# Two correction branches a tile instead of four in the context product of a fused Perceiver layer

## The reference, cut to what matters

```python
def _L0_xattn_ref(x1, x2, x1_scale, x1_zp, x2_scale, x2_zp):
    def fake_quant(x, scale, zp):
        s = scale.reshape(())
        z = zp.reshape(())
        q = jnp.clip(jnp.round(x / s + z), QMIN, QMAX)
        return (q - z) * s
    q1 = fake_quant(x1, x1_scale, x1_zp)
    q2 = fake_quant(x2, x2_scale, x2_zp)
    return jnp.matmul(q1, q2)
...
x = x + _L0_xattn_ref(_layernorm(x, axis=-1), ctx_4096, L0_xattn_x1_scale, L0_xattn_x1_zp, L0_xattn_x2_scale, L0_xattn_x2_zp)
x = x + _L0_attn_ref(_layernorm(x, axis=-1), L0_attn_Wqkv, L0_attn_Wo)
x = x + _L0_ffn_ref(_layernorm(x, axis=-1), L0_ffn_weight, L0_ffn_bias, L0_ffn_gate_w, L0_ffn_in_channel_scale, L0_ffn_out_channel_scale)
```

## Time and profile before

| | us |
|---|---|
| median of three runs | 401.46 (401.28 to 401.50) |
| the profiled execution, its own time | 400.98 |
| its span, first instruction to last | 399.2 |
| PE busy | 357.8 (90%) |
| DVE busy | 312.6 (78%) |
| ACT busy | 254.0 (64%) |
| POOL busy | 133.2 (33%) |
| DMA, bytes moved | 91.56 MB, 229 GB/s on average |

### The profile page before, as it was taken

One profiled execution on the slowest core, in us unless ns is written; L12 is line 12 of the kernel. 1 busy time (PEld: TensorE's weight loads), 2 busy tenths in 40 slices (PEclk: granted clock), 3 DMA queues, 4 the chain that ended last, 5 costly groups with the idle time before them and its releaser, 6 DMA issues.

```text
span 399.2 us, 9987 instructions
## 1 busy us (share of the span) xinstructions
PE 357.8 (90%) x4141; PEld 231.7 (58%) x4141; DVE 312.6 (78%) x592; ACT 254.0 (64%) x306; POOL 133.2 (33%) x148
## 2 busy tenths in 40 slices
PE   0437967999789999999999999999999999999996
PEld 0113943774344784569655965588457847955444
DVE  6898798998946689768985898679867997584753
ACT  3857885866788767864886577675878365233221
POOL 5320033415241224512471236213722246143051
PEclk9999999999999999999999999999999999999999
DMA  7999999479999579775867576757685200100002
GB/s 303 410 372 410 408 406 409 142 262 411 312 407 367 220 203 410 298 227 128 316 222 248 154 270 221 298 159 259 245 315 159 30 2 2 57 0 2 2 2 105
DMA packets 30243, 91.56 MB, mean 229 GB/s; under 512 B 8112, under 2 KB 8496, under 8 KB 30192
## 3 DMA queue, kind: packets, MB, share of 16 engines
q1 hardware_dynamic: 28320, 84.42, 58.9%
q10 hardware_dynamic: 1872, 6.40, 4.2%
HBM read 85.05 MB, written 4.19 MB: 224 GB/s over the span
## 4 chain that ended last, share of the span: by engine, by line
PE 56%; DVE 18%; DMA 9%; ACT 7%; SPq 4%; issue 3%; POOL 1%; DVEq 0%; ACTq 0%; POOLq 0%
DMA ring<-ctx 9%; PE R L1691 8%; PE T L1507 6%; PE R L1452 4%; ACT b L603 4%; PE R L1454 4%; PE R L1453 4%; PE R L1543 4%; PE C L1488 4%; PE R L1546 4%; PE R L1545 4%; SPq L380 2%; PE T L1590 2%; PE R L1574 2%; DVE st L1005 2%
## 5 line engine op out<-in xcount | busy, mean ns | idle before, releaser
L603 ACT ACTIVATE b<-ring,quant,qpar 128x2048 uint8<-128x2048 f32 x61 | 126.4, 2093 | 14.3 <-DMA ring<-ctx 8.2
L1543 PE MATMUL R<-T_hi,Wqkv_hi 128*128 128x128 f16 x448 | 77.8, 220 | 0.0
L1545 PE MATMUL R<-T_lo,Wqkv_hi 128*128 128x128 f16 x448 | 77.5, 220 | 0.0
L1546 PE MATMUL R<-T_hi,Wqkv_lo 128*128 128x128 f16 x448 | 77.5, 219 | 0.0
L1488 PE MATMUL C<-b,aT 128*64 128x512 f16 x256 | 36.1, 414 | 11.9 <-ACT b L603 5.9
L337 POOL TENSOR_TENSOR Pr<-Pr,mx 128x512 f32<-128x512 f32 x20 | 20.7, 1043 | 75.5 <-DVE mx L1109 75.5
L494 POOL TENSOR_TENSOR Pr<-Pr,mx 128x512 f32<-128x512 f32 x32 | 35.4, 1117 | 29.1 <-DVE mx L1115 29.1
L1543 PEld LDWEIGHTS R<-T_hi,Wqkv_hi 128*128 128x128 f16 x448 | 43.9, 98 | 2.0 <-issue 0.2
L1545 PEld LDWEIGHTS R<-T_lo,Wqkv_hi 128*128 128x128 f16 x448 | 43.8, 98 | 0.1
L1546 PEld LDWEIGHTS R<-T_hi,Wqkv_lo 128*128 128x128 f16 x448 | 43.8, 98 | 0.0
L1691 PE MATMUL R<-sgn,XS_hi 128*128 128x512 fp8e4 x96 | 36.6, 381 | 0.0
(11 more groups left out here) (172 smaller groups left out, 856.5 us busy)
## 6 DMA issues: line engine op xcount, KB each, us to landing
ring<-ctx SPq DMA_DIRECT2D x64, 1024.0 KB, 6.6
ring<-L_attn_Wo SPq DMA_DIRECT2D x4, 1024.0 KB, 9.3
ring<-L_ffn_weight SPq DMA_DIRECT2D x4, 1024.0 KB, 4.9
Wo<-L_attn_Wqkv SPq DMA_DIRECT2D x7, 544.0 KB, 15.4
X<-x ACTq DMA_DIRECT2D x6, 512.0 KB, 4.1
out<-X ACTq DMA_DIRECT2D x6, 512.0 KB, 6.1
X<-x SPq DMA_DIRECT2D x2, 512.0 KB, 11.3
sgn<-L_attn_Wqkv SPq DMA_DIRECT2D x1, 544.0 KB, 18.4
```

What stands on the lines that cost most here:

```text
L603: e.activation(b8[:, c % BRING, :], ring[:, slot, :], ACT.Identity, scale=qR2, bias=qZ2).then_inc(s_rf[slot], 1)
L1543: e.matmul(dst, hi, rows[0], start=k == 0 and g == 0, stop=False, skip_group_check=True)
L1545: e.matmul(dst, hi, rows[1], start=False, stop=False, skip_group_check=True)
L1546: last = e.matmul(dst, lo, rows[0], start=False, stop=k == KT - 1, skip_group_check=True)
```

## The change

The branch stands in the odd pairs only, and holds the correction for that pair and for the one before: 48 matmuls, where each of two branches held 24. So a pair's slots of `b16` may not be written again before the *next* pair has passed its branch, if the pair is even. The new function `read_by(t, c)` gives the count of `s_ctx` that `conv(t, c)` waits for. For pieces 6 and 7 it is 4t + 2 where it was 4t + 1; for pieces 4 and 5 it is 4(t-1) + 4 where it was 4(t-1) + 3; for 0 to 3 it is what it was.

```diff
+        def read_by(t, c):
+            return t * 4 + 2 if c >= BRING else (t - 1) * 4 + (2 if c // 2 == 1 else 4)
...
-                before = (t - 1) * 4 + 4 if c < 2 else (t - 1) * 4 + c // 2 + 1
-                at_least(e, s_ctx, before if c < BRING else t * 4 + 1)
+                at_least(e, s_ctx, read_by(t, c))
...
-                e.wait_ge(s_ctx, t * 4 + 1 if c >= BRING else (t - 1) * 4 + c // 2 + 1)
+                e.wait_ge(s_ctx, read_by(t, c))
...
-                def products(k, lhs, first, last):
+                def products(k, lhs, first, last, of_pair=pair):
...
-                                           b16[:, (2 * pair + b) % BRING, k, n * HALF:(n + 1) * HALF],
+                                           b16[:, (2 * of_pair + b) % BRING, k, n * HALF:(n + 1) * HALF],
...
                 products(0, rows(0), pair == 0, False)
-
-                with e.If_ne(uneven, 0):
-                    for k in range(2):
-                        for part in range(3):
-                            products(k, lambda b: zfrac[:, part, :], False, False)
+                if pair % 2 == 1:
+                    with e.If_ne(uneven, 0):
+                        for of_pair in (pair - 1, pair):
+                            for k in range(2):
+                                for part in range(3):
+                                    products(k, lambda b: zfrac[:, part, :], False, False, of_pair)
                 products(1, rows(1), False, pair == 3).then_inc(s_ctx, 1)
```

## The result

| | before | after |
|---|---|---|
| median of 12 runs, us | 401.54 (400.36 to 402.64) | 402.53 (401.82 to 402.91) |
| ratio of the runs | | 1.0021, 95% interval 1.0012 to 1.0030 |
| profiled execution, us | 400.98 | 401.87 |
| its span, us | 399.2 | 400.0 |

The change costs 0.84 us by the ratio and 0.89 us by the two profiled executions; +0.75 us was forecast (402.2 us, range 401.3 to 402.9 us). With its interval (0.5 to 1.2 us), the effect is clear of no change, and it lies on the bound of 0.2% that divided the two likely cases. The time alone could not have told the forecast from the rival whose hole stays (+1.24 us): +0.84 us lies between them. The traces do.

A forecast was written before the change was run, and what follows sets the result against it. PE was taken to bound the kernel from tile 3 on, ACT and DVE before tile 3 and again in tile 7. 0.87 + 0.37 - 0.49 = +0.75 us gave a median of 402.21 us, range 401.3 to 402.9 us.

The forecast's parts named there:

- the two likely cases: Whole kernel: slower (chance 0.52) or the same (0.42), divided at about 0.2%, that is 0.80 us.
- the rival whose hole stays: The hole in pair 2 of tile 3 stays or one like it turns up elsewhere: 402.70 us; chance 0.14.
- Sixteen branches at zero: Taking out 16 of 32 branches on PE gains zero, as four matmuls ahead cover each jump; uncovered, 3.3 us.
- branches on the path: Rival: the 16 even pairs' branches cost PE 0.207 us each, so the kernel is faster, 398.9 us; chance 0.06.
- The rival of the longer jumps: Jumps over 48 matmuls in tiles 4 to 7 stop PE's sequencer, up to 3.9 us on top, 406.1 us; chance 0.05.
- Tile 2, +0.87 us: Piece 6 of tile 2 starts 0.87 us later on ACT, and the whole delay arrives on PE.
- the answer to the wait: A conversion starts 0.10 us after the context matmuls it waits for end, as read in tile 3.
- Tile 7, +0.37 us: Later conversions on ACT delay exp of tile 7, which is on the chain of waits, by 0.37 us.
- Tiles 3 to 6, zero: Piece 6 starts 0.87 us later there, but PE does not stop; sum zero, bounds zero and 0.1 us a tile.
- the cover as named: In tiles 4 to 6, 0.18 us are left between the last pt_lo and the pv matmuls that need it.
- The hole, -0.49 us: PE's stop behind the branch of pair 2 of tile 3, read as a late code block, goes away: -0.49 us.
- the bounds, -0.49 us and zero: Limits for the hole of tile 3: -0.49 us if it goes, zero if it moves or was of one execution.

The follow-up runs named there:

- the order: The kernel before with both XS_hi of tile 2 put ahead of piece 7's conversion on ACT; 401.02 us, ratio 0.9979.
- e5_own27: The changed kernel, but in tiles 2 and 7 each pair keeps its own branch and pieces 6 and 7 wait for pair 0 only; 400.71 us.
- e8_wait3: The kernel before, but in tiles 4 to 6 pieces 6 and 7 wait for three pairs in place of one; 407.86 us, ratio 1.0145.
- e2_nobranch: The kernel before without the zero-point correction, all 32 branches and their 768 matmuls, with the old waits; 400.78 us, ratio 0.9982.
- e4_short: The kernel before without the branch and correction of pair 1 of tile 0, code behind 50 instructions earlier; 403.16 us, ratio 1.0049.
- e3_split: The kernel before with each branch cut in two, one for each k, 64 in all; 401.25 us, ratio 0.9990.

## Why the prediction was right, point by point

**Sixteen branches at zero.** Right. 32 branches more (ratio 0.9990) and 32 fewer (0.9982, with the stops gone) bracket it, and neither is near the 3.3 or 6.6 us that branches on the path would have given. The rival of the longer jumps did not come either: at the median they take 268 and 222 ns for 207 ns, and neither trace of the changed kernel has a stop behind tile 2.

**Tile 2, +0.87 us.** Right: +0.89 us in the trace after and +0.90 us with the waits alone, counted from pair 1. 0.10 us for the answer to the wait was read off one row and held in all tiles. That the chain runs through `XS_hi` was shown from both sides: later by the change, earlier by the order.

**Tile 7, +0.37 us.** Right: +0.38 us. `e5_own27`, which gives both tiles their early start back, takes both back.

**Tiles 3 to 6, zero.** Right, with the cover as named: `pt_lo` of tile 4 ends 0.19 us ahead of the matmuls that need it (timelines of DVE and PE of the kernel after).

```profile
200.25 1.24 DVE L942 TENSOR_TENSOR PT_lo<-T,PT_hi 128x512 f16<-128x512 f32 x2
...
201.68 0.28 PE L1595 MATMUL T<-PT_hi,vbd_hi 128*64 128x256 f16 x2
```

200.25 + 1.24 = 201.49 us for 201.68 us; 0.18 us were forecast. `e8_wait3` shows what the zero is worth: beyond the cover each tile pays in full.

**The hole, -0.49 us.** Right in this pair of traces, where it is exact, but the size was luck; right in its cause as far as shown: it goes when the code moves by 50 instructions, it comes with the transfer of a block, and other kernels have such stops elsewhere. Two things about it were too simple. Its size is not fixed: 0.49 to 0.96 us in seven executions of kernels with that code or nearly that code (1.47 to 1.94 us for the pair). The trace that the sum was read from had the smallest, and the bounds, -0.49 us and zero, left out all that was found later. And the kernel before has a second such place, in tile 6, which its first trace did not show. Both stops together took 0.49, 1.31 and 0.86 us in the three traces of the kernel before, 0.89 us on average. With that the sum would be 0.89 + 0.38 - 0.89 = +0.38 us, half of the forecast and just below the interval of the runs (0.5 to 1.2 us); with the 0.7 us that `e2_nobranch` and `e5_own27` give for the stops it is +0.6 us, within it. So the sign and the parts in tiles 2 and 7 stand, but that +0.75 us met +0.84 us so closely is in part chance.

**Left open**: that the stop *is* the block's late arrival rests on the moved code, the 1582 ns jump and the times of the transfers; the way from the end of a transfer to the next instruction was not taken apart, and neither was what the skipped code adds. Nor was it tried whether the transfers of the context on the same DMA engines make the block late. By the Trainium skill ("Runtime: NRT & Kernel Launch", Instruction fetch mechanics) crossing such a block is mostly hidden and a jump out of the window is what stalls. The holes in pair 2 of tile 3 and in pair 1 of tile 6 fit that, being in or just behind a jump; the two stops of `e4_short` came 3 us behind the last one.

## What to carry to other kernels

Count a branch by what the engine's array does meanwhile, not by its duration: here 0.2 us of sequencer time stood under 0.43 us of matmuls and was worth nothing. To free a buffer one step later is not free for the instructions *behind* the one that waits; look them up on its engine, at the first and last passes of a loop above all, where nothing else is the bound. When a kernel is within half a percent, a change in code size alone may be worth as much as the change one meant to make, and the same kernel's stops differ by 0.8 us from one execution to the next. Profile both kernels more than once, and compare with a variant of the same size in instructions.

## What the runs showed of the hardware that was not expected

Leaving out one branch and 24 matmuls that are never executed made the kernel 0.49% slower (`e4_short`), by two stops of PE of 1.0 to 1.1 us in other places and by 3.41 us at half the granted clock behind the first. A jump takes 207 ns as a rule, but 1582 ns once, in `e3_split`, where the chain has its hole. A stop of 1.4 us on PE in `e8_wait3` was followed by 4 us at a granted clock of 0.58 (3.41 us of them at 1.2 GHz, the rest at 2.4 GHz), once in three such stops; the other two kept the full clock.
